# Expert stage of a decoder layer: down products turned round, weights stationary and 512 tokens moving

## The reference

```python
logits = x @ gate_w.T                       # x is the layer-normed input, (3584, 256)
scores = sigmoid(logits)
# 2 of 4 groups of experts by score + bias, then 4 of the 8 experts; weights normalised, times 2.5
cw = ...                                    # (3584, 8), zero for experts not chosen
g = einsum('nh,ehi->eni', x, Wg)            # 8 experts, H = 256, I = 128
u = einsum('nh,ehi->eni', x, Wu)
y = einsum('eni,eih->enh', silu(g) * u, Wd)
out = einsum('enh,ne->nh', y, cw) + (silu(x @ Wg_s) * (x @ Wu_s)) @ Wd_s
x_out = x_before_norm + out
```

## Time and profile before

| | |
|---|---|
| Median of three runs | 758.57 us (756.07 to 758.85) |
| The profiled execution, its span | 759.8 us, 758.0 us |
| PE busy over the span | 699.2 us (92%) |
| DVE, ACT, POOL busy | 500.4, 408.3, 347.4 us (66%, 54%, 46%) |
| Mean granted clock of PE, as a share of 2.4 GHz | 0.983 |
| First matmul of the shared expert, groups 0 to 6 | 444.45, 506.38, 547.83, 589.48, 630.45, 671.56, 712.17 us |

### The profile page before, as it was taken

How to read it: one execution, slowest core, us unless ns; L and a number is a source line. 1 busy time by engine, 2 the same in 40 slices (tenths; PEclk the granted TensorE clock), 3 DMA queues, 4 the chain that set the end, 5 groups by cost and what they waited for, 6 DMA issues and landing times. The chain is left out here.

```text
span 758.0 us, 13311 instructions
## 1 busy us (share of the span) xinstructions
PE 699.2 (92%) x4496; PEld 616.8 (81%) x4496; DVE 500.4 (66%) x1232; ACT 408.3 (54%) x923; POOL 347.4 (46%) x482
## 2 busy tenths in 40 slices
PE   3879999999999999999999865989999999999997
PEld 2768888988988898889888854878888888888886
DVE  5686685775875866758758654766576667666442
ACT  4855766776776768567767532524243333333321
POOL 2756846765657558557575311323222223232222
PEclk9989999999999999999999998999999999999999
DMA  7622322313213313223001057022221203121200
GB/s 215 180 87 69 117 69 66 108 38 98 88 48 88 98 47 99 65 70 117 24 22 37 18 148 266 1 112 83 112 84 58 108 31 138 55 112 57 112 29 29
DMA packets 50769, 64.47 MB, mean 85 GB/s; under 512 B 3801, under 2 KB 49417, under 8 KB 49841
## 3 DMA queue, kind: packets, MB, share of 16 engines
q1 hardware_dynamic: 50736, 64.06, 26.7%
HBM read 56.60 MB, written 7.45 MB: 85 GB/s over the span
## 5 line engine op out<-in xcount | busy, mean ns | idle before, releaser
L1440 POOL TENSOR_TENSOR sg<-sg,cw_wide 128x512 f32<-128x512 f32 x56 | 74.6, 1331 | 187.9 <-ACT sg L1397 177.7
L1401 ACT ACTIVATE a_hi<-af 128x512 fp32r<-128x512 f32 x63 | 39.8, 632 | 157.4 <-DVE af L1521 157.4
L76 PE MATMUL bank<-h_hi,w_lo 128*128 128x512 f32 x224 | 92.6, 413 | 6.9 <-DVE w_lo L1538 5.1
L77 PE MATMUL bank<-h_lo,w_hi 128*128 128x512 f32 x224 | 90.5, 404 | 0.0
L78 PE MATMUL bank<-h_hi,w_hi 128*128 128x512 f32 x224 | 89.6, 400 | 0.0
L822 POOL TENSOR_TENSOR ctxt_lo<-ctxtf,ctxt_hi 128x375 fp32r<-128x375 f32 x64 | 58.4, 933 | 64.3 <-ACT ctx_hi L609 56.2
L1521 DVE TENSOR_TENSOR af<-bank,sg 128x512 f32<-128x512 f32 x63 | 43.2, 686 | 65.0 <-POOL sg L1440 61.9
L1526 DVE TENSOR_TENSOR a_lo<-af,a_hi 128x512 fp32r<-128x512 f32 x63 | 47.2, 749 | 34.9 <-ACT a_hi L1401 34.9
L827 POOL TENSOR_TENSOR ctx_lo<-ctxf,ctx_hi 125x256 fp32r<-125x256 f32 x96 | 68.9, 746 | 0.0
L76 PE MATMUL bank<-w_hi,a_lo 128*128 128x256 f32 x224 | 63.3, 283 | 0.0
L77 PE MATMUL bank<-w_lo,a_hi 128*128 128x256 f32 x224 | 63.2, 282 | 0.0
(11 more groups left out here) (252 smaller groups left out, 2293.3 us busy)
## 6 DMA issues: line engine op xcount, KB each, us to landing
cw_wide<-cw_scratch SPq DMA_DIRECT2D x7, 2048.0 KB, 7.1
ctxtf<-in_ctx_t SPq DMA_DIRECT2D x32, 375.0 KB
ctxf<-in_ctx SPq DMA_DIRECT2D x32, 375.0 KB
xt<-in_x SPq DMA_DIRECT2D x8, 448.0 KB, 3.7
x_scratch<-x2b SPq DMA_DIRECT2D x8, 448.0 KB, 3.2
x2n<-x_scratch SPq DMA_DIRECT2D x7, 512.0 KB, 4.7
x2t<-x_scratch SPq DMA_DIRECT2D x7, 512.0 KB, 3.9
out_dram<-x2t SPq DMA_DIRECT2D x7, 512.0 KB, 2.9
```

What stands on the lines that cost most here:

```text
L76: pe.matmul(dst, a_lo, b_hi, start=first, stop=False, **kw)
L77: pe.matmul(dst, a_hi, b_lo, start=False, stop=False, **kw)
L1401: act.activation(a_hi[n % (AHEAD + 1)][:, :], af[(p + n) % 2][:, :], ACT.Copy).then_inc(a_hi_ok, 1)
L1440: pool.tensor_tensor(sg[b][:, :], sg[b][:, :], cw_wide[p][:, ORDER[n], :], ALU.mult).then_inc(sgw_ok, 1)
```

## The change

The down products are turned round. In `down_columns` the down weights are stationary (two blocks of 128 features) and all 512 tokens move: 2 blocks times 3 parts is 6 matmuls of 512 columns. The sum then stands in `y_bank` with features on the partitions. It has to be turned back: ACT copies both banks to SBUF (`copy_y`, at step 1 of the next group), PE turns them in eight 128x128 transposes into `h_bank` (`turn_y`, at step 4 of the next group, behind its down product), and DVE's `finish` reads `h_bank` in place of `y_bank`, at step 5 in place of step 1. As `h_bank[0]` is written again by `turn_cw` at step 6, PE waits there for `finish` (`out_ok`). The last group keeps the old form for its own down products (`down_rows`), and finishes from `y_bank`. A one-element memset ahead of the stage sets the first count of `t_y`.

```diff
+            yt = [sb(f"yt{h}", [P, FFN_TOKENS]) for h in range(KB)]
...
-                def down(g, n):
+                def down_rows(g, n):
                     e, b = ORDER[n], n % (AHEAD + 1)
                     pe.wait_ge(a_lo_ok, NE * g + n + 1)
-                    if n == 0 and not is_first(g):
-                        pe.wait_ge(out_ok, 2 * g)
+                    if n == 0:
+                        pe.wait_ge(yt_ok, KB * g)
...
+                def down_columns(g, n):
+                    e, b = ORDER[n], n % (AHEAD + 1)
+                    pe.wait_ge(a_lo_ok, NE * g + n + 1)
+                    if n == 0 and not is_first(g):
+                        pe.wait_ge(yt_ok, KB * g)
+                    for h in range(KB):
+                        w = slice(GU + h * P, GU + (h + 1) * P)
+                        last = mm3(pe, y_bank[h][:, :], w_hi[e][:, w], w_lo[e][:, w], a_hi[b][:, :], a_lo[b][:, :], n == 0, n == NE - 1)
+                    if n == NE - 1:
+                        last.then_inc(y_mm, 1)
+
+                def turn_y(g, last):
+                    pe.wait_ge(yt_ok, KB * (g + 1))
+                    pe.wait_ge(cwt_ok, g + 2)
+                    if not last:
+                        pe.wait_ge(lg2_ok, g + 3)
+                    for t in range(T):
+                        for h in range(KB):
+                            turned = pe.transpose(h_bank[t // 2][:, (t % 2) * D + h * P:(t % 2) * D + (h + 1) * P],
+                                                  yt[h][:, t * P:(t + 1) * P], ident[:, :])
+                    turned.then_inc(t_y, 1)
+
                 def group(g, p, last):
+                    down = down_rows if last else down_columns
...
                         elif not is_first(g):
-                            down(g - 1, NE + n - AHEAD)
+                            down_columns(g - 1, NE + n - AHEAD)
                         if n == 1 and not last:
                             turn_h3(pe, g + 1)
+                        if n == 4 and not is_first(g):
+                            turn_y(g - 1, last)
                         if n == 6 and not last:
+                            if not is_first(g):
+                                pe.wait_ge(out_ok, 2 * g)
                             turn_cw(g + 1)
...
+                def copy_y(g):
+                    act.wait_ge(y_mm, g + 1)
+                    act.wait_ge(t_y, g + 1)
+                    for h in range(KB):
+                        act.activation(yt[h][:, :], y_bank[h][:, :], ACT.Copy).then_inc(yt_ok, 1)
...
                             if n == 1:
+                                if not is_first(g):
+                                    copy_y(g - 1)
                                 h3_high(act, g + 1, h3_hi[1 - p])
...
+                        elif n == 1:
+                            copy_y(g - 1)
                         act_high(g, p, n)
...
-                def finish(g, p, nth):
-                    dve.wait_ge(y_mm, g + 1)
+                def finish(g, p, nth, source):
+                    if source is y_bank:
+                        dve.wait_ge(y_mm, g + 1)
+                    else:
+                        dve.wait_ge(t_y, g + 2)
...
-                        if n == 1 and not is_first(g):
-                            finish(g - 1, 1 - p, nth)
+                        if n == 5 and not is_first(g):
+                            finish(g - 1, 1 - p, nth, h_bank)
```

More of the change, by code:

```diff
@@ L1251, in decoder_layer @@
             y_mm, out_ok = sem("down_product"), sem("out_ready")
+            yt_ok, t_y = sem("down_columns_copied"), sem("down_transposed")
             out_g = out.rearrange("b l d -> (b l) d").rearrange("(t p) d -> p t d", p=P)
@@ L1374, in _ @@
                 for n in range(NE - AHEAD, NE):
-                    down(NG2 - 1, n)
+                    down_rows(NG2 - 1, n)
             @block.scalar
@@ L1532, in finish @@
                         x2q = x2t[p][:, 2 * q:2 * q + 2, :]
-                        dve.tensor_tensor(x2q, y_bank[q][:, :].rearrange("p (t d) -> p t d", t=2), x2q, ALU.add).then_inc(out_ok, 1)
+                        dve.tensor_tensor(x2q, source[q][:, :].rearrange("p (t d) -> p t d", t=2), x2q, ALU.add).then_inc(out_ok, 1)
                 def split_low(n):
@@ L1559, in group @@
                             route_experts(g + 1)
+                dve.memset(held[:, 0:1], 0.0).then_inc(t_y, 1)
                 dve.wait_ge(wk_in, 48)
@@ L1571, in _ @@
                 group(NG2 - 1, 0, NG2 // 2, True)
-                finish(NG2 - 1, 0, NG2 // 2 + 1)
+                finish(NG2 - 1, 0, NG2 // 2 + 1, y_bank)
 def kernel(**inputs):
```

## The result

The changed kernel took 763.18 us (median of seven runs, 762.56 to 765.02) against 758.67 us for the kernel before on the same chip (seven runs, 756.07 to 761.75). The ratio is 1.0066, with a 95% interval of 1.0045 to 1.0086: +4.5 us where +8.3 was forecast, slower and inside the range. One execution of late_turn (803.33 us) and one of the kernel before (1339.01 us) stand far above all others and are left out of every median and ratio here.

A forecast was written before the change was run, and what follows sets the result against it. PE's stream bounds it from group 1 on, except step 7's gate_up, which waits for DVE's af behind the router. Terms: 8.5 + 0.96 - 1.2 = +8.3 us on 758.57, giving 766.9 us; range 761.5 to 771.

The forecast's parts named there:

- Finish at step 5: DVE's two adds delay PE's turn_cw and step 7's gate_up by 1.7 us in groups 1 to 5: +8.5 us.
- The turns: Eight PE transposes per group, 0.96 us: hidden in PE's wait in groups 1 to 5, +0.96 us in group 6.
- The wide products: Down products of 6 matmuls of 512 columns save 0.04 us each; 31 of 54 count: 1.2 us saved.
- the bound I had set aside: Down products: with a matmul's overhead halved at best, some 0.06 us saved per expert; 0.04 was taken.
- ACT's copies and SP's queue: ACT's copies at step 1 covered by slack, SP's later loads landing just in time: both cost zero.
- rival B: SP's broadcast of routing weights lands 2 us later, delaying POOL's step 1 and the router: +4 to +7.5 us; chance 0.09.
- The count of the queue: SP's small store takes 3.54 us until the broadcast issues at 631.1; it lands at 638.2, POOL needing it at 638.6.
- A: DVE's router escapes POOL's block (e_gt 0.42 for 1.51 us), finish off the path: +2.8 or +1.6 us; chance 0.15.
- C: PE's clock falls to 1.2 GHz after the wait and turns before step 7: +8.3 us if in five groups; chance 0.08.

The follow-up runs named there:

- late_turn: Changed kernel with turn_y and finish at step 7 behind turn_cw, no PE wait for finish there, SP's order altered to suit: 762.26 us, ratio 1.0055 to the kernel before.
- adds_in_old: Kernel before plus two spare DVE adds at step 5 of groups 1 to 5, PE waiting for them ahead of turn_cw: 766.51 us, ratio 1.0106.
- half_wait: Changed kernel with turn_cw waiting for only the first of finish's two adds: 762.06 us, ratio 1.0047 to the kernel before.
- sp_order: Changed kernel with SP issuing the norm load first, then store, routing weights, and x2t load last: 763.90 us, ratio 1.0084 to the kernel before.
- the second comparison: Changed kernel, unaltered, measured again against the kernel before on another chip: 765.89 us against 758.27, ratio 1.0113.
- old_no_wait: Kernel before with turn_cw behind step 7's gate_up and af of step 5 made inside the router: 757.50 us, ratio 0.9987; repeated, 754.99 us, 0.9950.
- turns_twice: Changed kernel with turn_y's eight transposes done twice (16): 764.68 us, ratio 1.0086 to the kernel before.

## Why the prediction was right, and where its sizes were off

The step that it rested on, that `finish` enters DVE's chain ahead of `turn_cw`, was right, and adds_in_old and half_wait show it by itself. The range held, but the forecast of +8.3 was nearly twice the +4.5 of the first comparison. Term by term:

- Finish at step 5: forecast 5 x 1.7 = 8.5, measured 7.75 from step 3 to 7 (and 7.35 by adds_in_old). Groups 2 to 5 grew by 1.77, 1.65, 1.62 and 1.56 us, group 1 by 1.15. The small turns take 0.35 us after a wait, not 0.46.
- The turns: forecast 0.96 each and hidden in groups 1 to 5; measured 0.88, hidden, and 0.89 more in group 6.
- The wide products: forecast 0.04 per expert and 1.2 us in all; measured 1.8 over 24 steps from 7 to 3. This term was sized too small. Down products are 1.36 to 1.40 us long for 1.43, so 0.06 and 1.4 in all, which was the bound I had set aside; of the rest some 0.25 is `gate_up`, which in groups 1, 3 and 5 ran at 2.72 for 2.75, and 0.16 the turns of `h`. In group 3, at 620 us above, the sixth and first of a down product are (620.18 - 619.05) / 5 = 0.226 us apart (start 619.05 in the same timeline). The 0.2325 that I had taken over from gate and up is that of group 4; in group 3 they have 0.229 before and 0.226 after.
- ACT's copies and SP's queue: forecast zero; measured zero with the cover shown. POOL did wait for `cw_wide` in groups 2 to 5, which I had named as the sign of rival B; the sign came and the cost did not (sp_order), so as a sign it was no good. The count of the queue was too short: the small store took 3.93 us until the broadcast was issued, for the 3.54 that I took from group 0, and POOL in group 4 started 0.6 us behind its silu.

SP's issues in group 3, and POOL's multiply of step 1 in group 4:

```profile
626.18 0.40 SPq L1268 DMA_DIRECT2D cw_scratch<-cwt  x1
630.11 0.35 SPq L1272 DMA_DIRECT2D cw_wide<-cw_scratch  x1
```

```profile
637.50 1.30 POOL L1479 TENSOR_TENSOR sg<-sg,cw_wide 128x512 f32<-128x512 f32 x1 [2.12 <-DMA cw_wide<-cw_scratch]
```

Summed over what the change touches from group 1 on, 7.75 + 0.89 - 1.80 = 6.8 us against 8.3. The rest of the distance to the 4.5 of the first comparison is not in these terms: the second comparison gave 7.6. The profiled executions differ in what the change doesn't touch: over the 13 traces the expert stage starts between 442.05 and 446.32 us. The time of an execution mostly goes with its mean granted clock: of the twelve in the first comparison of old_no_wait the three fastest (753.5 to 754.0 us) have 0.986, the three slowest (758.3 to 758.9) 0.978 to 0.981. In the traces the clock is low in two places while PE works, between 40 and 80 us of the launch and in group 0; between 40 and 80 us its mean was 0.87 before and 0.96 in the changed kernel. No run here was made to part this from the change, so the 2.3 us between 6.8 and 4.5 stay open.

Of the rivals, A did not happen in the changed kernel, and turns_twice, where its shift came, refuted its worth; B fell by sp_order; C did not happen: from group 1 to PE's last matmul the granted clock of the changed kernel is 1.00, with waits of up to 1.7 us and 0.35 of turns behind them. By the Trainium skill ("TensorE: Matmul & The Clock Gate", Part 4), by which transposes do not count as busy in the same way, up to 2.1 us were quiet here, and the clock held; whether they count is not shown, as no run tells the two apart.

## What to carry to other kernels

Where two engines keep step, find every place at which the waiting one is released by the other with nothing to spare, and count how far each is from being late: here a 1.3 us move on DVE, not PE's matmuls, set the price, and the down products made shorter on PE alone, 63 by 0.06 us, were worth nothing that could be measured. A wait placed ahead of a small instruction holds back everything queued behind it; first ask whether the instruction can stand behind the next large block, and whether it needs all of what it waits for (half_wait took half of the loss of 7.6 us away by one number). To size a suspected wait, put it into the old kernel by itself.

## What the runs showed of the hardware that was not expected

- Moving a DVE instruction that a POOL multiply blocks ahead of the multiply makes that one cheap (`e_gt` 0.42 us for 1.51), but not the chain: in turns_twice the next but one took the block, 1.40 us for 0.42, and the chain as a whole gained 0.15 us.
- Whether DVE's layer norm and a POOL multiply meet is worth 1 us, and a small shift decides it. The four instructions of the norm took 2.46 us in group 3 of the kernel before, where the multiply began among them, and 1.38 to 1.39 in groups 2 to 5 of the changed kernel. There POOL waited for the late weights, but that isn't the reason: in sp_order it did not, and the norm took 1.38 to 1.39 all the same, because the multiply came behind it. In group 1 it was the other way round, 1.38 before and 2.48 changed. DVE and POOL, group 3 of before, then group 4 of sp_order:

```profile
595.35 2.46 DVE L164 TENSOR_SCALAR h<-x2n,mv,r 128x256 f32<-128x256 f32 x4 [0.92 <-POOL r L145]
596.05 1.29 POOL L1440 TENSOR_TENSOR sg<-sg,cw_wide 128x512 f32<-128x512 f32 x1 [0.83 <-ACT sg L1397]
```

```profile
636.09 1.39 DVE L164 TENSOR_SCALAR h<-x2n,mv,r 128x256 f32<-128x256 f32 x4 [1.01 <-POOL r L145]
637.61 1.62 POOL L1480 TENSOR_TENSOR sg<-sg,cw_wide 128x512 f32<-128x512 f32 x1 [1.65 <-ACT sg L1427]
```

- Matmuls of the same form, 128x128 stationary and 512 columns moving, do not have one spacing. Gate and up of the routed experts run at 0.229 us (before) or 0.226 (changed) in groups 1, 3 and 5, and at 0.233 or 0.234 in groups 2, 4 and 6 of both kernels. Odd and even groups differ in the buffers that they use; which buffer makes the difference was not tried.
